# Second attention: stack fills from POOL's queue, and a new written order for each engine's step

## The chip, the cores and the metric

The kernel runs on one core of a Trainium2 chip. A core has a matrix engine (TensorE, here PE), a vector engine (VectorE, DVE), a scalar engine (ScalarE, ACT), a general engine (GpSimd, POOL) and a sync engine (SyncE, SP), which issues most of the DMAs. Each engine works through its own list of instructions in order and waits on semaphores. DMAs issued by SP go into a hardware queue, those issued by POOL into a software queue; both are served by the core's 16 DMA engines. The metric is the time of one execution on the device in microseconds (us), lower is better.

## The reference

Two transformer layers on x of (16, 256, 128), in float32. Each layer normalises x and adds an attention and a mixture of experts. The change lies in the second layer's attention, 16 heads of 8 channels with relative positions clipped at 64 both in the scores and in the values:

```python
dist = jnp.clip(idx[None, :] - idx[:, None], -R, R) + R
pe_k = rel_emb_k[dist]
pe_v = rel_emb_v[dist]
qkv = (x @ W_qkv + b_qkv).reshape(b, s, 3, H, hd)
...
q = q / jnp.sqrt(jnp.asarray(hd, x.dtype))
score = jnp.einsum('bhqd,bhkd->bhqk', q, k) + jnp.einsum('bhqd,qkd->bhqk', q, pe_k)
attn = jax.nn.softmax(score, axis=-1)
ctx = jnp.einsum('bhqk,bhkd->bhqd', attn, v) + jnp.einsum('bhqk,qkd->bhqd', attn, pe_v)
ctx = jnp.transpose(ctx, (0, 2, 1, 3)).reshape(b, s, d)
return ctx @ W_out + b_out
```

The layer's result is x plus this attention plus the experts' output; the experts' rows lie in DRAM (`eo`) when the attention begins, and each token gathers its two rows and adds them with their gates.

## The kernel before

Four stages follow one another: a front stage (first experts, about 0 to 100 us), the first attention (to about 825 us), the second experts (`ffn1_stage`, to about 1100 us) and the second attention (`attn1_stage`, L1331, to the end).

The second attention handles 16 batches of 256 tokens in 32 steps, one for each tile of 128 queries. `steps` (L1374) writes them all out, four to a round r; `tile_of` (L1380) gives the tile within its batch (`it`, 0 or 1) and which of two stack buffers holds the batch (`par`). A step works on eight head pairs (`hp`), and several tiles are in flight at a time:

- PE (`step`, L1499) computes for tile s the key scores of each head pair (`key_scores`, L1428, into the two buffers `ps_S`), for the next tile s+1 the relative scores (`rel_scores`, L1421, into the one buffer `ps_R`), then the transposes of the finished exponentials (`transposes`, L1437, two buffers `ps_T`). For the tile before, s-1, it computes the relative values (`rel_values`, L1446, four quarters in two buffers), the values weighed with the probabilities (`weigh`, L1469), the folds (`folds`, L1480) that add the picked relative values, and the transposed reciprocals (`reciprocals`, L1489); for s-2 the output projection (`project_out`, L1495). Once per batch come `project_qk` (L1405, in it = 1) and `project_v` (L1412, in it = 0).
- ACT (`step`, L1578) copies the relative scores out (`keep_R`, L1553), takes the exponentials (`exponentials`, L1561), copies every second transposed pair (`keep_T`, L1572), the reciprocals (`keep_rdT`) and the projected q and k (`keep_qk`).
- DVE (`step`, L1673) adds key scores and the skewed relative scores and takes the minimum (`add_scores`, L1615), copies the other transposed pairs (`keep_T`, L1667), picks the diagonals of the relative values (`pick_diagonal`, L1630), inverts the sums (`invert`), divides (`divide`), adds the projection (`add_y`) and the two gathered expert rows (`combine`, L1649), and stores the values of a batch (`keep_v`, L1603).
- POOL (`step`, L1736) copies x for project_v (`copy_x`), gathers the expert rows of tile s-2 by two indirect DMAs (`gather`, L1724, after the combine of the tile before), and in it = 1 splits q and k of two batches on into three bf16 parts (`split_qk`, L1247).
- SP (`step`, L1778) sends each quarter of the relative scores to DRAM (`send_band`, L1760, `skew`) and fetches it back shifted by a row's place (`fetch_band`, L1767, into `Sb`); it stores results, sends the parts (`send_parts`, L1266, in it = 1, after the fills of the batch before have landed) and, in it = 0, fills the stacks.

A stack holds q and k of a batch as 72 rows of bf16 (nine products of parts of eight channels): `stack_queries` (L1274) and `stack_keys` (L1283) are three DMAs each of 24 rows of 8 KB from DRAM, 192 KB a DMA, issued for the next batch once its parts are in DRAM. The queries are needed by the relative scores one step on, the keys two steps on. What releases a buffer matters for the order: keep_R of a quarter waits until the same quarter of the tile before has been fetched back, and `combine` waits for both gathers of its tile. The order before is a loop over the head pairs in each engine, with the other work hung on single pairs:

```python
for hp in range(HP):
    if it == 0 and hp == 0:
        pe.wait_ge(keys_in[par], (r + 1) * KSTACK)
    key_scores(s, it, par, hp)
    ...
    rel_scores(s + 1, nit, npar, hp)
    if hp >= LAG:
        transposes(s, hp - LAG)
```

In the expert stage SP also sends the first batch's parts and fills its stacks (`experts`, L1041), while POOL splits the first two batches' q and k and then stores the experts' outputs (L1064).

Of the kernel before, what the change touches and what calls it, by code (L numbers as in the profile page):

```python
# [1001 lines left out]
def ffn1_stage(nc, w0_d, w1_d, wo_d, slots_dram, eo_dram, xn_all, send_ids, sent, ident, x_all, b_out, xnT_all, front, parts, one, bias_q, bias_k):  # L1002
# [11 lines left out]
    with Pool(nc) as m:  # L1014
# [23 lines left out]
        with nc.Block() as block:  # L1038
            @block.sync
            def _(sp):  # L1040
                def experts(half, r):  # L1041
                    for i in range(2):
                        e = r * 2 + i
                        g = slice(half * GH, (half + 1) * GH)
                        sp.wait_ge(o_done, up(half * E + e - 1))
                        sp.dma_start(w[i][:, 0:HID], w0_d[bass.ds(e, 1)]).then_inc(loaded[i], 16)
                        sp.dma_start(w[i][:, VALUE:VALUE + full], w1_d[bass.ds(e, 1), :, 0:full]).then_inc(loaded[i], 16)
                        sp.dma_start(w[i][:, HID + PAD:VALUE], w1_d[bass.ds(e, 1), :, full:HID]).then_inc(loaded[i], 16)
                        sp.dma_start(wo[i][:, 0:HC - 1, :], wo_d[bass.ds(e, 1), 0:full].rearrange("a (c p) d -> p (a c) d", p=P)).then_inc(loaded[i], 16)
                        sp.dma_start(wo[i][UP, HC - 1, :], wo_d[bass.ds(e, 1), full:HID]).then_inc(loaded[i], 16)  # L1050
                        sp.dma_start(xe[i][:, :, :], xs_v[bass.ds(e, 1), :, g, :]).then_inc(loaded[i], 16)
                    if half == 0 and isinstance(r, int):

                        send_parts(sp, front, parts, 0)
                        stack_queries(sp, front, parts, 0, 0)
                        stack_keys(sp, front, parts, 0, 0)

                sp.wait_ge(cleared, 1)
                sp.wait_ge(sent[0], 16 * NT)
                rolled(sp, E // 2, lambda r: experts(0, r))  # L1060
                sp.wait_ge(sent[1], 16 * NT)
                rolled(sp, E // 2, lambda r: experts(1, r))

            @block.gpsimd  # L1064
            def _(pool):
                def experts(half, r):
                    for i in range(2):
                        e = r * 2 + i
                        pool.wait_ge(o_ready, half * E + e + 1)
                        pool.dma_start(eo_v[bass.ds(e, 1), :, half * GH:(half + 1) * GH, :], eo[i][:, :, :]).then_inc(stored[i], 16)  # L1070

                scatter(nc, slots_dram, xn_all, send_ids, 1, range(NT - 2 * TPG, NT - TPG), sent)
                for k in range(2):
                    scatter(nc, slots_dram, xn_all, send_ids, k, range(NT - TPG, NT), sent)
                split_qk(nc.gpsimd, pool, front, one, 0, front.sm["qk_ready"], 1)
                nc.gpsimd.tensor_tensor(x_all[:, :, :], x_all[:, :, :], bc(b_out[:, :], 1, NT), ALU.add).then_inc(biased, 1)
                split_qk(nc.gpsimd, pool, front, one, 1, front.sm["parts_out"], PSENDS)
                pool.wait_ge(sent[1], 16 * NT)
                for half in range(2):
                    rolled(pool, E // 2, lambda r: experts(half, r))  # L1080
                pool.wait_ge(biased, 1)
                for i in range(2):
                    pool.wait_ge(stored[i], 16 * PAIRS1)
# [104 lines left out]
HP = H1 // 2  # L1188
# [11 lines left out]
QUAD = 4  # L1200
# [130 lines left out]
def attn1_stage(nc, front, x_all, xnT_all, a, gates, slot_ids, ident, one, bias_q, bias_k, bias_v, rel_st, tabs, pick, fold):  # L1331
# [6 lines left out]
    LAG = 2  # L1338
    RING = 4
    with Pool(nc) as m:  # L1340
# [61 lines left out]
        with nc.Block() as block:  # L1402
            @block.tensor
            def _(pe):
# [94 lines left out]
                def step(r, i):  # L1499
                    s = r * 4 + i  # L1500
                    it, par = tile_of(i)
                    nit, npar = tile_of(i + 1)
                    pit = 1 - it
                    behind = tiles_behind(r, i)
                    prev_b = r * 2 + par - (1 if it == 0 else 0)
                    for hp in range(HP):
                        if it == 0 and hp == 0:
                            pe.wait_ge(keys_in[par], (r + 1) * KSTACK)
                        key_scores(s, it, par, hp)
                        if it == 1 and hp == 0:  # L1510
                            pe.wait_ge(queries_in[npar], (r + 1 + (1 if i == 3 else 0)) * QSTACK)
                        rel_scores(s + 1, nit, npar, hp)
                        if hp >= LAG:
                            transposes(s, hp - LAG)
                        elif behind >= 1:
                            transposes(s - 1, hp + HP - LAG)
                        if it == 1 and hp == 1:
                            project_qk(r * 2 + par + 2)
                        if behind >= 2 and hp == 1:
                            project_out(s - 2)  # L1520
                        if behind >= 1:
                            if hp == 2:
                                reciprocals(s - 1)
                            if hp in (3, 5):
                                rel_values(s - 1, prev_b, pit, hp - 3)
                                rel_values(s - 1, prev_b, pit, hp - 2)
                            if hp == 4:
                                for q in range(QUAD):
                                    weigh(s - 1, prev_b, pit, q)
                            if hp == 7:  # L1530
                                folds(s - 1)
                        if it == 0 and hp == 7:
                            project_v(r * 2 + par)

                pe.wait_ge(sm["cleared"], 1)
                pe.wait_ge(sm["loaded"], 16 * 3)
# [16 lines left out]
            def _(act):  # L1553
# [24 lines left out]
                def step(r, i):  # L1578
                    s = r * 4 + i
                    it, par = tile_of(i)  # L1580
                    behind = tiles_behind(r, i)
                    for hp in range(HP):
                        keep_R(s + 1, hp)
                        exponentials(s, it, hp)
                        if hp % 2 == 0:
                            if hp >= LAG:
                                keep_T(s, it, hp - LAG)
                            elif behind >= 1:
                                keep_T(s - 1, 1 - it, hp + HP - LAG)
                        if behind >= 1 and hp == 2:  # L1590
                            keep_rdT(s - 1)
                        if it == 1 and hp == 1:
                            keep_qk(nc, act, front, ps_p, bias_q, bias_k, r * 2 + par + 2)

                for hp in range(HP):
                    keep_R(0, hp)
# [5 lines left out]
            def _(v):  # L1602
# [70 lines left out]
                def step(r, i):  # L1673
                    s = r * 4 + i
                    it, par = tile_of(i)
                    behind = tiles_behind(r, i)
                    for hp in range(HP):
                        add_scores(r, i, hp)
                        if hp == 0:
                            if behind >= 2:  # L1680
                                divide(s - 2)
                            if it == 1:
                                keep_v(r * 2 + par)
                        if hp == 1 and behind >= 1:
                            invert(s - 1, 1 - it)
                        if hp % 2 == 1:
                            if hp >= LAG:
                                keep_T(s, it, hp - LAG)
                            elif behind >= 1:
                                keep_T(s - 1, 1 - it, hp + HP - LAG)  # L1690
                        if hp == 1 and behind >= 2:
                            add_y(s - 2)
                        if behind >= 1 and 3 <= hp < 7:
                            pick_diagonal(s - 1, 1 - it, hp - 3)
                        if hp == 7 and behind >= 2:
                            combine(s - 2)

                nc.vector.memset(vx[:, :, :, :, :], 0.0)
                nc.vector.memset(ps_X0[:, :, :, :], 0.0)
# [18 lines left out]
            def _(pool):  # L1718
# [15 lines left out]
                            in_offset=bass.IndirectOffsetOnAxis(ap=ids[:, k, :], axis=0)).then_inc(sm["rows_in"], 16)  # L1734

                def step(r, i):  # L1736
                    it, par = tile_of(i)
                    if it == 1:

                        copy_x(r * 2 + par + 1)  # L1740
                    if tiles_behind(r, i) >= 2:
                        gather(r * 4 + i - 2)
                    if it == 1:

                        split_qk(nc.gpsimd, pool, front, one, r * 2 + par + 2, sm["parts_out"], (r * 2 + par + 2) * PSENDS)
# [9 lines left out]
            def _(sp):  # L1755
# [22 lines left out]
                def step(r, i):  # L1778
# [1 line left out]
                    it, par = tile_of(i)  # L1780
                    nit, npar = tile_of(i + 1)

                    if it == 0:
                        stack_queries(sp, front, parts, r * 2 + par + 1, 1 - par)
                    send_band(s + 1, nit, 0)
                    fetch_band(s, it, 3)
                    if s >= 3:
                        store(s - 3)
                    if it == 0:
                        stack_keys(sp, front, parts, r * 2 + par + 1, 1 - par)  # L1790
                    send_band(s + 1, nit, 1)
                    fetch_band(s + 1, nit, 0)
                    if it == 1:
# [105 lines left out]
```

## Time and profile before

| | |
|---|---|
| median of 3 runs | 1667.84 us (1659.12 to 1680.68) |
| profiled execution, its own time | 1669.93 us |
| its span, first to last instruction | 1668.3 us |
| mean granted TensorE clock | 0.972 of full speed |
| PE busy over the span | 1513.7 us (91%) |
| DVE busy | 905.4 us (54%) |
| ACT busy | 729.8 us (44%) |
| POOL busy | 300.3 us (18%) |
| hardware queue (SP) | 169.54 MB, 39.0% of the 16 DMA engines' span |
| software queue (POOL) | 12.44 MB, 2.6% |

Times in the trace are counted from the first instruction, in us. A busy PE counts from the start of a matmul to its modelled end, and matmuls overlap; where a number should say how long PE needs, the chain's pieces or the distance of two starts is used. An idle time stands in brackets in front of the instruction that ended it, with what ended it.

### The profile page before, as it was taken

The numbers are of one execution on the slowest core, as the hardware profiler recorded it, in microseconds if no ns is written. First come the engines' busy times: TensorE is split into PE (matmuls) and PEld (weight loads), VectorE is DVE, ScalarE is ACT, GpSimd is POOL, SyncE is SP. The second block draws the span as 40 slices with busy tenths as digits, with TensorE's granted clock in tenths as the row PEclk, the third lists the DMA queues.
The fourth block names the chain that finished last, engine by engine and source line by source line (L and its number), as shares of the span: only waits on it lengthen the run. The fifth ranks groups of instructions, "written<-read, shape, count | busy, mean of one in ns | idle before, by whom it ended". The sixth has DMA issues, their size and how long they took to land. (4 is left out here: it accounts for less than half of the span.)

```text
span 1668.3 us, 37746 instructions
## 1 busy us (share of the span) xinstructions
PE 1513.7 (91%) x13904; PEld 1216.0 (73%) x13912; DVE 905.4 (54%) x3195; ACT 729.8 (44%) x1975; POOL 300.3 (18%) x383
## 2 busy tenths in 40 slices
PE   6899999999999999999599999948898989888987
PEld 5568888888888888888365656527677777766776
DVE  5336545454545454545322222226778787767786
ACT  2322222222222222222232232338788888878885
POOL 2011201111010101010440000002333233223333
PEclk9999999999999999999799999968999999999999
DMA  4009400000000000000243232248889998888996
GB/s 119 0 7 86 105 9 8 8 6 7 3 9 3 9 2 10 0 13 1 88 118 114 76 114 76 83 119 230 251 251 259 257 265 258 237 257 232 262 257 200
DMA packets 214008, 183.80 MB, mean 110 GB/s; under 512 B 83275, under 2 KB 203749, under 8 KB 211420
## 3 DMA queue, kind: packets, MB, share of 16 engines
q1 hardware_dynamic: 208494, 169.54, 39.0%
q0 software_dynamic: 5376, 12.44, 2.6%
q8 instruction: 85, 1.39, 0.4%
q14 instruction: 53, 0.43, 0.1%
HBM read 103.63 MB, written 78.14 MB: 109 GB/s over the span
## 5 line engine op out<-in xcount | busy, mean ns | idle before, releaser
L1564 ACT ACTIVATE a1Pm<-a1Pm,a1nmx 128x256 f32<-128x256 f32 x512 | 255.6, 504 | 0.0
L1626 DVE CUSTOM_DVE_ANT_0 a1Pm<-a1ps_S,a1Sb 128x256 f32<-128x256 f32 x512 | 195.9, 420 | 77.6 <-issue 61.2
L775 DVE TENSOR_TENSOR a0AT<-a0ps_AM,mask 128x384 f32<-128x384 f32 x256 | 124.9, 549 | 192.0 <-PE a0ps_AM L595 191.8
L780 DVE TENSOR_TENSOR a0MT<-a0ps_AM,mask 128x384 f32<-128x384 f32 x256 | 138.3, 554 | 87.4 <-PE a0ps_AM L616 86.8
L1559 ACT ACTIVATE a1Rt<-a1ps_R 128x384 f32<-128x384 f32 x264 | 127.9, 485 | 111.1 <-PE a1ps_R L1424 78.3
L1443 PE MATMUL a1ps_T<-ident,a1Pm 128*128 128x128 f32 x1024 | 158.9, 278 | 0.3 <-ACT a1Pm L1564 0.3
L1169 DVE TENSOR_TENSOR f1hid<-f1ge,f1ps_b 128x512 f32<-128x512 f32 x80 | 55.0, 687 | 192.0 <-PE f1ps_b L1102 184.4
L614 PE MATMUL a0ps_AM<-a0AT 128*128 128x256 f32 x512 | 152.9, 380 | 0.0
L1424 PE MATMUL a1ps_R<-rel_st,a1stk 72*128 72x192 bf16 x528 | 91.7, 257 | 65.0 <-ACT a1Rt L1559 49.2
L579 PE MATMUL a0ps_qk<-xnT_all,a0w_in 128*128 (+1 forms) x512 | 138.3, 393 | 2.0 <-PEq L151 1.3
L722 ACT ACTIVATE a0qk<-a0ps_qk 128x512 f32<-128x512 f32 x128 | 76.4, 597 | 116.5 <-PE a0ps_qk L579 116.5
L726 ACT ACTIVATE a0v<-a0ps_v 128x512 f32<-128x512 f32 x64 | 38.2, 597 | 190.6 <-PE a0ps_v L605 190.6
L1443 PEld LDWEIGHTS a1ps_T<-ident,a1Pm 128*128 128x128 f32 x1024 | 117.4, 144 | 0.9 <-ACT a1Pm L1564 0.6
L1424 PEld LDWEIGHTS a1ps_R<-rel_st,a1stk 72*128 72x128 bf16 x528 | 41.7, 99 | 103.6 <-ACT a1Rt L1559 83.1
L730 ACT ACTIVATE a0oT<-a0ps_o 128x512 f32<-128x512 f32 x64 | 38.2, 597 | 171.4 <-PE a0ps_o L628 171.4
L615 PEld LDWEIGHTS a0ps_AM<-a0AT 128*128 128x128 f32 x512 | 97.3, 190 | 13.2
L1112 PE MATMUL f1ps_o<-f1wo,f1hid 128*128 128x128 f32 x768 | 90.0, 277 | 16.4 <-DVE f1hid L1169 16.4
L1433 PE MATMUL a1ps_S<-a1stk 72*128 72x256 bf16 x512 | 102.2, 282 | 0.0
L1112 PEld LDWEIGHTS f1ps_o<-f1wo,f1hid 128*128 128x128 f32 x768 | 87.0, 192 | 20.7 <-DVE f1hid L1169 13.1
L579 PEld LDWEIGHTS a0ps_qk<-xnT_all,a0w_in 128*128 128x128 f32 x512 | 87.1, 190 | 19.9 <-issue 12.1
L1100 PE MATMUL f1ps_a<-f1xT,f1w 128*128 128x512 f32 x192 | 99.8, 602 | 0.7 <-ACT f1xT L1132 0.7
L1564 ACT ACTIVATION_READ_ACCUMULATOR a1Pm<-a1Pm,a1nmx 128x1 f32 x512 | 99.4, 194 | 0.0
(249 smaller groups left out, 2988.9 us busy)
## 6 DMA issues: line engine op xcount, KB each, us to landing
skew<-a1Rt SPq DMA_DIRECT2D x132, 384.0 KB, 5.0
a1Sb<-skew SPq DMA_DIRECT2D x131, 384.0 KB, 5.6
a1stk<-parts_q SPq DMA_DIRECT2D x51, 192.0 KB
a1stk<-parts_k SPq DMA_DIRECT2D x51, 192.0 KB
f1w<-in_L_ffn_w_kernel SPq DMA_DIRECT2D x16, 344.0 KB, 2.9
f1w<-in_L_ffn_w_kernel SPq DMA_DIRECT2D x16, 320.0 KB, 3.2
f1wo<-in_L_ffn_wo_kernel SPq DMA_DIRECT2D x16, 320.0 KB, 4.2
slots<-zeros SPq DMA_DIRECT2D x8, 512.0 KB, 15.0
```

What stands on the lines that cost most here:

```text
L579: ins = nc.tensor.matmul(ps_qk[:, i, :], w_in[:, i, p * P:(p + 1) * P], xnT_all[:, bass.ds(b * T, T)], start=True, stop=True)
L614: nc.tensor.matmul(M[:, 0:T], S[:, 0:P], S[:, 0:T], start=True, stop=True)
L775: nc.vector.tensor_tensor(AT[i][h][:, :], ps_AM[i][h][:, 0:HB], mask[:, :], ALU.mult).then_inc(A_ready, 1)
L780: nc.vector.tensor_tensor(MT[i][h][:, :], ps_AM[i][h][:, 0:HB], mask[:, :], ALU.mult).then_inc(M_ready, 1)
L1100: nc.tensor.matmul(ps_a[u % 2][:, :], w[i][:, u * P:(u + 1) * P], xT[i][:, :], start=True, stop=True).then_inc(a_done, 1)
L1112: ins = nc.tensor.matmul(ps_o[i][:, s, :], hid[:, c, s * P:(s + 1) * P], wo[i][:, c, :], start=(c == 0), stop=(c == HC - 1))
L1424: ins = nc.tensor.matmul(ps_R[:, n, :], stk[par][:, 0, 2 * hp + n, it * P:(it + 1) * P], rel_st[:, it, :], start=True, stop=True)
L1433: ins = nc.tensor.matmul(ps_S[hp % 2][:, n, :], stk[par][:, 0, h, it * P:(it + 1) * P], stk[par][:, 1, h, :], start=True, stop=True)
L1443: ins = nc.tensor.transpose(ps_T[k % 2][:, n, jt, :], Pm[:, place(2 * k + n), jt * P:(jt + 1) * P], ident[:, :])
L1559: nc.scalar.activation(Rt[:, hp, :, :], ps_R[:, :, :].rearrange("p n c -> p c n"), ACT.Copy).then_inc(sm["R_ready"], 1)
L1564: nc.scalar.activation(Pm[:, place(h), :], Pm[:, place(h), :], ACT.Exp, bias=nmx[it][:, h:h + 1], scale=-1.0, accum_out=den[it][:, h:h + 1 ...
L1626: nc.vector.tensor_tensor_reduce(out=Pm[:, place(h), :], in0=ps_S[hp % 2][:, n, :], in1=bias_of(it, hp, n), scale=-1.0, scalar=3.0e38, op0 ...
```

## The change

The six stack fills of a batch move from SP's list to POOL's: in each step with it = 0 POOL waits until the step before has finished its key scores (S_done) and then issues them, ahead of the gather of that step. The first batch's fills move to POOL in the expert stage. PE, ACT and DVE keep their instructions; the loop over head pairs is replaced by a list written out line by line, with relative scores and relative values earlier, and on DVE `divide` first and `combine` between the additions of pairs 3 and 4. The helper functions stay as they are. The diff, with the removed loops cut:

```diff
--- before.py
+++ after.py
@@ -1052,8 +1052,6 @@
         if half == 0 and isinstance(r, int):
 
             send_parts(sp, front, parts, 0)
-            stack_queries(sp, front, parts, 0, 0)
-            stack_keys(sp, front, parts, 0, 0)
 
     sp.wait_ge(cleared, 1)
     sp.wait_ge(sent[0], 16 * NT)
@@ -1075,6 +1073,8 @@
     split_qk(nc.gpsimd, pool, front, one, 0, front.sm["qk_ready"], 1)
     nc.gpsimd.tensor_tensor(x_all[:, :, :], x_all[:, :, :], bc(b_out[:, :], 1, NT), ALU.add).then_inc(biased, 1)
     split_qk(nc.gpsimd, pool, front, one, 1, front.sm["parts_out"], PSENDS)
+    stack_queries(pool, front, parts, 0, 0)
+    stack_keys(pool, front, parts, 0, 0)
     pool.wait_ge(sent[1], 16 * NT)
     for half in range(2):
         rolled(pool, E // 2, lambda r: experts(half, r))
@@ -1500,37 +1500,57 @@
         s = r * 4 + i
         it, par = tile_of(i)
         nit, npar = tile_of(i + 1)
-        pit = 1 - it
+        b = r * 2 + par
+        prev_b = b - (1 if it == 0 else 0)
         behind = tiles_behind(r, i)
-        prev_b = r * 2 + par - (1 if it == 0 else 0)
-        for hp in range(HP):
-            if it == 0 and hp == 0:
...
+        if it == 0:
+            pe.wait_ge(keys_in[par], (r + 1) * KSTACK)
+        key_scores(s, it, par, 0)
+        if it == 1:
+            pe.wait_ge(queries_in[npar], (r + 1 + (1 if i == 3 else 0)) * QSTACK)
+        rel_scores(s + 1, nit, npar, 0)
+        if behind >= 1:
+            transposes(s - 1, 6)
+        key_scores(s, it, par, 1)
+        if behind >= 1:
+            transposes(s - 1, 7)
+        rel_scores(s + 1, nit, npar, 1)
+        if it == 1:
+            project_qk(b + 2)
+        key_scores(s, it, par, 2)
+        rel_scores(s + 1, nit, npar, 2)
+        if behind >= 2:
+            project_out(s - 2)
+        if behind >= 1:
+            rel_values(s - 1, prev_b, 1 - it, 0)
+            rel_values(s - 1, prev_b, 1 - it, 1)
+        transposes(s, 0)
+        rel_scores(s + 1, nit, npar, 3)
+        key_scores(s, it, par, 3)
+        transposes(s, 1)
+        if behind >= 1:
+            reciprocals(s - 1)
+            rel_values(s - 1, prev_b, 1 - it, 2)
+            rel_values(s - 1, prev_b, 1 - it, 3)
+        key_scores(s, it, par, 4)
+        key_scores(s, it, par, 5)
+        rel_scores(s + 1, nit, npar, 4)
+        transposes(s, 2)
+        transposes(s, 3)
+        rel_scores(s + 1, nit, npar, 5)
+        if behind >= 1:
+            for q in range(QUAD):
+                weigh(s - 1, prev_b, 1 - it, q)
+        rel_scores(s + 1, nit, npar, 6)
+        key_scores(s, it, par, 6)
+        transposes(s, 4)
+        transposes(s, 5)
+        rel_scores(s + 1, nit, npar, 7)
+        key_scores(s, it, par, 7)
+        if it == 0:
+            project_v(b)
+        if behind >= 1:
+            folds(s - 1)
 
     pe.wait_ge(sm["cleared"], 1)
     pe.wait_ge(sm["loaded"], 16 * 3)
@@ -1578,19 +1598,33 @@
     def step(r, i):
         s = r * 4 + i
         it, par = tile_of(i)
+        b = r * 2 + par
         behind = tiles_behind(r, i)
-        for hp in range(HP):
-            keep_R(s + 1, hp)
-            exponentials(s, it, hp)
...
+        keep_R(s + 1, 0)
+        if behind >= 1:
+            keep_T(s - 1, 1 - it, 6)
+        keep_R(s + 1, 1)
+        exponentials(s, it, 0)
+        if it == 1:
+            keep_qk(nc, act, front, ps_p, bias_q, bias_k, b + 2)
+        exponentials(s, it, 1)
+        keep_R(s + 1, 2)
+        keep_R(s + 1, 3)
+        exponentials(s, it, 2)
+        if behind >= 1:
+            keep_rdT(s - 1)
+        keep_T(s, it, 0)
+        exponentials(s, it, 3)
+        keep_R(s + 1, 4)
+        keep_T(s, it, 2)
+        keep_R(s + 1, 5)
+        exponentials(s, it, 4)
+        exponentials(s, it, 5)
+        keep_R(s + 1, 6)
+        keep_T(s, it, 4)
+        keep_R(s + 1, 7)
+        exponentials(s, it, 6)
+        exponentials(s, it, 7)
 
     for hp in range(HP):
         keep_R(0, hp)
@@ -1673,27 +1707,38 @@
     def step(r, i):
         s = r * 4 + i
         it, par = tile_of(i)
+        b = r * 2 + par
         behind = tiles_behind(r, i)
-        for hp in range(HP):
-            add_scores(r, i, hp)
-            if hp == 0:
...
+        if behind >= 2:
+            divide(s - 2)
+        if it == 1:
+            keep_v(b)
+        add_scores(r, i, 0)
+        if behind >= 1:
+            keep_T(s - 1, 1 - it, 7)
+            invert(s - 1, 1 - it)
+        add_scores(r, i, 1)
+        if behind >= 1:
+            pick_diagonal(s - 1, 1 - it, 0)
+        add_scores(r, i, 2)
+        if behind >= 2:
+            add_y(s - 2)
+        if behind >= 1:
+            pick_diagonal(s - 1, 1 - it, 1)
+        add_scores(r, i, 3)
+        keep_T(s, it, 1)
+        if behind >= 1:
+            pick_diagonal(s - 1, 1 - it, 2)
+        if behind >= 2:
+            combine(s - 2)
+        add_scores(r, i, 4)
+        add_scores(r, i, 5)
+        if behind >= 1:
+            pick_diagonal(s - 1, 1 - it, 3)
+        keep_T(s, it, 3)
+        add_scores(r, i, 6)
+        keep_T(s, it, 5)
+        add_scores(r, i, 7)
 
     nc.vector.memset(vx[:, :, :, :, :], 0.0)
     nc.vector.memset(ps_X0[:, :, :, :], 0.0)
@@ -1734,12 +1779,18 @@
                 in_offset=bass.IndirectOffsetOnAxis(ap=ids[:, k, :], axis=0)).then_inc(sm["rows_in"], 16)
 
     def step(r, i):
+        s = r * 4 + i
         it, par = tile_of(i)
+        if it == 0:
+            if s > 0:
+                pool.wait_ge(sm["S_done"], s * HP)
+            stack_queries(pool, front, parts, r * 2 + par + 1, 1 - par)
+            stack_keys(pool, front, parts, r * 2 + par + 1, 1 - par)
         if it == 1:
 
             copy_x(r * 2 + par + 1)
         if tiles_behind(r, i) >= 2:
-            gather(r * 4 + i - 2)
+            gather(s - 2)
         if it == 1:
 
             split_qk(nc.gpsimd, pool, front, one, r * 2 + par + 2, sm["parts_out"], (r * 2 + par + 2) * PSENDS)
@@ -1780,14 +1831,10 @@
         it, par = tile_of(i)
         nit, npar = tile_of(i + 1)
 
-        if it == 0:
-            stack_queries(sp, front, parts, r * 2 + par + 1, 1 - par)
         send_band(s + 1, nit, 0)
         fetch_band(s, it, 3)
         if s >= 3:
             store(s - 3)
-        if it == 0:
-            stack_keys(sp, front, parts, r * 2 + par + 1, 1 - par)
         send_band(s + 1, nit, 1)
         fetch_band(s + 1, nit, 0)
         if it == 1:
```

## Rows read from the trace of the kernel before

**Rows 1.** The chain that ended last: start us, us, what.

```profile
1178.76 1.88 PE a1ps_c L1477 x64
...
1590.48 7.71 DMA skew<-a1Rt
1598.20 6.46 DMA a1Sb<-skew
1612.14 1.88 PE a1ps_c L1477 x64
...
1644.50 1.88 PE a1ps_c L1477 x64
```

**Rows 2.** Stretches: us, PE, PEld, DVE, ACT, POOL busy, clock, DMA share, GB/s.

```profile
1300.00:1400.00 100.00, 91.28 (x1340) 73.47 (x1338) 79.92 (x357) 85.29 (x285) 32.05 (x45) 1.00 0.92 261
```

**Rows 3.** The chain within 1300 to 1345 us, pieces of PE.

```profile
1313.31 1.02 PE a1ps_X L1465 x16
1314.34 0.87 PE a1ps_p L1465 x16
...
1332.42 1.08 PE a1ps_c L1485 x32
...
1334.14 0.22 PE a1ps_S L1433 x2
1334.36 0.17 PE a1ps_R L1424 x2
1334.52 0.44 PE a1ps_T L1443 x4
```

**Rows 4.** Timeline of ACT: start us, us, engine, line, out<-in, count [idle before].

```profile
1604.75 0.49 ACT L1559 ACTIVATE a1Rt<-a1ps_R 128x384 f32<-128x384 f32 x1 [1.56 <-DMA a1Sb<-skew]
1605.16 0.51 ACT L1564 ACTIVATE a1Pm<-a1Pm,a1nmx 128x256 f32<-128x256 f32 x1
...
1606.16 0.57 ACT L1575 ACTIVATE a1PT<-a1ps_T 128x512 f32<-128x512 f32 x1
```

**Rows 5.** Timeline of DVE.

```profile
1587.38 0.73 DVE L1657 SCALAR_TENSOR_TENSOR x_all<-a1rows,gates,x_all 128x128 f32<-128x128 f32 x2
...
1597.72 0.42 DVE L1626 CUSTOM_DVE_ANT_0 a1Pm<-a1ps_S,a1Sb 128x256 f32<-128x256 f32 x1 [1.31 <-issue]
...
1598.41 0.69 DVE L1670 COPY a1PT<-a1ps_T 128x512 f32<-128x512 f32 x1
1599.01 0.68 DVE L1636 TENSOR_TENSOR a1X<-a1ps_X,pick 128x512 f32<-128x512 f32 x1
```

**Rows 6.** DMA issues of the page: out<-in, queue, count, KB each, median us to landing.

```profile
skew<-a1Rt SPq DMA_DIRECT2D x132, 384.0 KB, 5.0
a1Sb<-skew SPq DMA_DIRECT2D x131, 384.0 KB, 5.6
```

**Rows 7.** Timeline of PE.

```profile
1597.28 0.39 PE L1433 MATMUL a1ps_S<-a1stk 72*128 72x256 bf16 x2
```

**Rows 8.** Timeline of POOL.

```profile
1576.44 1.04 POOL L1255 TENSOR_TENSOR a1prt<-a1qkf,one 128x512 bf16<-128x512 f32 x1 [1.50 <-ACT a1qkf L1244]
...
1581.17 1.04 POOL L1255 TENSOR_TENSOR a1prt<-a1low,one 128x512 bf16<-128x512 f32 x1
...
1603.37 0.17 POOL L1727 COPY a1ids<-slot_ids 128x2 uint32<-128x2 uint32 x1
...
1605.26 0.95 POOL L1732 DMA_INDIRECT a1rows<-eo,a1ids  x1 [0.30 <-issue]
```

**Rows 9.** Timeline of SP's queue.

```profile
1249.22 0.47 SPq L1271 DMA_DIRECT2D parts_k<-a1prt  x1
...
1253.34 1.44 SPq L1280 DMA_DIRECT2D a1stk<-parts_q  x3
```

**Rows 10.** The line of POOL's plain DMA: duration ns min/median/max, first and last start.

```profile
L1070 POOL DMA_DIRECT2D eo<-f1eo x16: 750/750/857, 852.0 to 1093.8; - x16
```

**Rows 11.** The line of POOL's gather, from its issue.

```profile
DMA to landing us min/median/max: 2.5/5.3/9.6
```

More of the change, by code:

```diff
@@ L1502, in step @@
                     nit, npar = tile_of(i + 1)
-                    pit = 1 - it
+                    b = r * 2 + par
+                    prev_b = b - (1 if it == 0 else 0)
                     behind = tiles_behind(r, i)
-                    prev_b = r * 2 + par - (1 if it == 0 else 0)
-                    for hp in range(HP):
-                        if it == 0 and hp == 0:
[L1508 to L1533, printed above, removed]
@@ L1580, in step @@
                     it, par = tile_of(i)
+                    b = r * 2 + par
                     behind = tiles_behind(r, i)
-                    for hp in range(HP):
-                        keep_R(s + 1, hp)
-                        exponentials(s, it, hp)
[L1585 to L1593, printed above, removed]
+                    keep_R(s + 1, 0)
[23 more added lines that the diff above has]
+                    exponentials(s, it, 7)
                 for hp in range(HP):
@@ L1675, in step @@
                     it, par = tile_of(i)
+                    b = r * 2 + par
                     behind = tiles_behind(r, i)
-                    for hp in range(HP):
-                        add_scores(r, i, hp)
-                        if hp == 0:
[L1680 to L1696, printed above, removed]
+                    if behind >= 2:
+                        divide(s - 2)
```

## The prediction

> **What bounds the kernel now.** The change lies in the second attention, so I read that stage first. The chain of waits gives its pace: the weighing (64 matmuls, 1.88 us) starts at 1178.76 and, 28 steps later, at 1644.50 [rows 1]. That is 465.74 / 14 = 33.27 us for a pair of steps (one batch), 16.6 a step. The table of stretches shows in a quiet 100 us PE busy 91.28, ACT 85.29, DVE 79.92, and the DMA engines at a share of 0.92 [rows 2]. No engine is full by itself, and the reader should expect the bound in the hand-overs between engines that each work through a fixed list.
>
> The chain's pieces tell how long PE really needs, since each counts until the next one's start: key scores S 0.22, relative scores R 0.17, transposes T 0.44, two relative values 1.02 + 0.87, folds 1.08 [rows 3], weighing 1.88 [rows 1]. With eight each of S, R and T, the second pair of relative values at about half (an estimate: half the matmuls) and a projection (from the folds at 1332.42 to the key scores at 1334.14 are 1.72, which leaves 0.64 [rows 3]) a step needs some 13.5 us of PE. ACT: a pair of exponentials E takes 1.00 (1605.16 to 1606.16), a keep_R 0.41 before it, a keep_T some 0.5 [rows 4]; 8 x 1.41 + 4 x 0.5 + 0.4 for what is small is 13.7. DVE: a pair of score additions 0.69, a keep_T 0.60, a pick the same by its length, combine 0.73 [rows 5]; with what is small some 13.2. Each needs about 13.5 and the step takes 16.6: 3 us a step are waits for another list.
>
> One of the waits is for DMAs. At 1604.75 a step's first keep_R had sat idle 1.56 us for a band fetch [rows 4]. The chain shows why: that band went out at 1590.48, took 7.71, and came back in 6.46 [rows 1], where the medians of the two DMAs are 5.0 and 5.6 [rows 6]. SP issues the 1.1 MB of stack fills around it.
>
> **The new order, laid out.** No instruction of PE, ACT or DVE is added or removed, so a gain must come from waits. I lay out a first-tile step from its first key scores (time 0) with the durations above (the number behind a letter is the head pair). A hand-over costs 0.4 to 0.6 from the start of the producing instruction: key scores at 1597.28 [rows 7], their addition at 1597.72 [rows 5].
> PE: T6 of the tile before at 0.4, T7 at 1.4 (after the last exponentials), R1 1.8, R2 2.8, first relative values 3.1 to 5.0, T0 5.0, R3 5.5, T1 5.9, second relative values 6.4 to 7.5, S4 and S5 to 7.9, T2 8.1, T3 8.9, weighing 9.5 to 11.4, T4 and T5 to 12.7, S7 to 13.1, project_v to 13.6, folds to 14.6.
> ACT: keep_R0 1.3, keep_R1 2.2, E0 2.6, E1 3.6, keep_R2 4.5, keep_R3 5.9 (0.9 idle, for R3), E2 6.2, E3 7.8, keep_R4 8.8, keep_R5 9.7, E4 10.1, E5 11.1, keep_R6 12.1, E6 13.4, E7 to 15.4.
> DVE: addition 0.5, keep_T7 2.0, invert 2.6, addition 3.0, pick 4.2, addition 4.8, pick 5.8, addition 6.4, keep_T1 7.2, pick 7.8, **combine 8.4**, additions 9.1 and 9.9, pick 10.7, the last addition to 14.3.
> So 14.64 us. The second-tile step, with keep_v ahead on DVE and the projection of q and k ahead of S2, comes out at 14.51 by the same working and ends with ACT 1.3 us past PE's end, as the first began. A pair takes 29.15; for the small gaps between PE's groups, left out above, I add 0.4: 29.55. Against 33.27 that is 3.7 us a pair, if nothing else moves.
>
> **What the POOL queue costs.** In a first-tile step POOL now waits for the key scores of the step before (0.9 before time 0) and for the parts in DRAM, issues six stack fills, and only then gathers the expert rows that combine wants at 8.4. Before, nothing stood ahead of that gather. The parts: by the layout the split starts 4.0 into the second-tile step; it lasts from 1576.44 to the end of the row at 1581.17, 5.8 [rows 8], so SP sends the parts from 9.8, the last at 10.7. They land at the latest 4.1 later by the closest pair (parts at 1249.22, stack at 1253.34 [rows 9]), which is 0.3 past the next time 0; a fuller queue may make it 2.1. I take 0.8.
> A stack fill on POOL is not in the trace. The nearest row is the only plain DMA that POOL issues, eo, 0.75 [rows 10]. Below it I allow 0.3 (fewer and longer runs, 24 rows of 8 KB); above it, by the gather's row of 0.95 [rows 8], 0.95. I take 0.75 and 0.1 between: six end at 0.8 + 5.1 = 5.9. The gather's ids follow, and its second DMA starts 1.9 later (1603.37 to 1605.26 [rows 8]), at 7.8. Gathers land 2.5 to 9.6 after their issue, median 5.3 [rows 11], and they now also stand behind the stack data in the same queue. I take 3.9, midway between least and median, since the fills have had 7 us to drain: 11.7. Combine is wanted at 8.4, and DVE has 0.6 to spare there (its next addition ends its part 0.6 before E4 can begin). DVE stands still, and with it E4, T4 and all behind: 11.7 - 8.4 - 0.6 = 2.7 us a pair. Bounds: fills at 0.3 with a landing of 2.5 bring the rows at 0.8 + 1.8 + 1.9 + 2.5 = 7.0, no wait; parts at 2.1, fills at 0.85 with their gap and a landing of 5.3 bring them at 14.4, a wait of 5.4.
> The bands: from keep_R1's end to the next step's keep_R0 took 14.3 before (1590.48 to 1604.75 [rows 1, 4]); the layout leaves 12.8, so unchanged latencies would stall 1.5 a pair. The wait at combine comes ahead of that point and covers it. It costs what it says if that cover is gone (rival 2).
>
> **The sum.** 29.55 + 2.7 = 32.25 a pair. The old mean of 33.27 lies 0.9 above a quiet pair (1612.14 to 1644.50 is 32.36 [rows 1]), for late DMAs; as the hardware queue loses the fills and the wait at combine covers such delays, I add none (all of it back would be 14 us). Gain 1.02 x 16 pairs = 16 us. The first batch's fills, now on POOL in the expert stage, cost nothing: POOL's first store there would go out 5 us later (six at 0.85), and its buffer is next needed an expert or two on. What they cost without that cover is those 5 us, once. The profiled run took 1669.9 (span 1668.3), 2.1 above the median of 1667.8: 1669.9 - 16 gives 1654, and I forecast 1653.
>
> **Rivals.**
> 1. No wait at combine, and fast bands. Fills at 0.3 let the gather land before 9.0, and bands at their medians, 5.0 + 5.6 [rows 6], fit into 12.8. Pair 29.55, gain 3.7 x 16 = 60: 1610. For it: POOL is busy 32 of 100 us [rows 2]. Against it: the 0.75 row.
> 2. No wait at combine, but the bands keep their 7.7 and 6.5 beside the fills: pair 29.55 + 1.5 = 31.05, gain 2.2 x 16 = 35: 1635. For it: the bytes stay, and the DMA share is 0.92 in a longer step [rows 2]. Against it again the 0.75 row. Beside it stands a rule of the Trainium skill, "DMA: Bandwidth & Descriptors", section Issuing engines are not separate DMA queues: DMAs of all issuers run on the same 16 DMA engines and interleave, and issuing from several saves only issue time. By that rule moving the fills does not speed the bands; no run here shows it yet.
> 3. The gather comes so late that the kernel is slower. Its place is combine in each first-tile step, its price 5.4 by the bound above: 29.55 + 5.4 = 34.95, 1.7 more than now, x 16 = +27: 1697. It decides from rows landing later than 8.4 + 0.6 + 3.7 = 12.7. For it: landings up to 9.6 occur [rows 11], and the gather stands behind 1.1 MB. Against it: those 7 us.
>
> **How the numbers follow.** Forecast 0.45, rival 1 0.18, rival 2 0.17, rival 3 0.20. The forecast's own range is 1630 to 1675: a landing 1.2 earlier or later moves it by 19. A change of 2% (33 us: below 1634 or above 1701) is about what a measurement of this kernel can tell. Faster by that: rival 1 whole, half of rival 2, a twentieth of the forecast: 0.30. Slower: somewhat over half of rival 3, whose waits can also be longer: 0.12. Same: 0.58. The range leaves out a tenth at each end: 1612 to 1694.
>
> **What would show it.** Right: in first-tile steps DVE idles 2 to 3 us before combine for the DMA of a1rows, in nearly all of them; a fill takes POOL 0.75; second-tile steps take 14.5 to 15; ACT's idle time for a1Sb shrinks. Wrong: no idle time ahead of combine (rivals 1 and 2, told apart by ACT's waits for a1Sb), fills far from 0.75, or steps over 15.5 without a wait at combine, which would put the error into my layout.

## The result and the profile after

The changed kernel takes 1710.18 us (median of 4 runs), the one before 1669.64, measured beside it: a ratio of 1.0241 (95% interval 1.0199 to 1.0284). It is slower by 2.4%, past the upper end of the predicted range (1694). The profiled execution, the longest of the four, took 1720.68 with a span of 1719.1.

The row of stretches that answers to [rows 2] (same columns):

```profile
1300.00:1400.00 100.00, 82.99 (x1095) 68.03 (x1094) 68.63 (x300) 72.89 (x239) 35.29 (x55) 0.90 0.85 227
```

PE, DVE and ACT each do less in 100 us (1095 PE instructions for 1340; over 1150 to 1650 us 5895 for 6444), the granted clock is 0.90 instead of 1.00, and the DMA engines are less busy. So all of them wait more. For whom, the waits over 1150 to 1700 us say (engine, line, whom it waited for: us in all, times, longest):

```profile
DVE x_all L1691 <- DMA a1rows<-eo,a1ids: 81.9, 15, 7.2
...
POOL a1stk L1280 <- PE a1ps_S L1433: 43.5, 9, 5.7
```

and over 1150 to 1650 us, with the bands, the kernel before first:

```profile
ACT a1Rt L1559 <- DMA a1Sb<-skew: 26.1, 18, 4.1
```

```profile
ACT a1Rt L1579 <- DMA a1Sb<-skew: 31.6, 7, 4.9
```

The first row is DVE ahead of `combine`: 81.9 / 15 = 5.5 us in nearly every batch; the kernel before has no such wait in this stretch. The last is ACT waiting for a band: 7 times instead of 18, but 4.5 us each instead of 1.5. The second, POOL's own, is the time for which it stands idle until its fills may go. One batch on POOL's timeline, with DVE's row of the same batch below it:

```profile
1299.94 1.60 POOL L1280 DMA_DIRECT2D a1stk<-parts_q  x3 [5.52 <-PE a1ps_S L1433]
1301.52 1.48 POOL L1289 DMA_DIRECT2D a1stk<-parts_k  x3
1303.63 1.04 POOL L1777 DMA_INDIRECT a1rows<-eo,a1ids  x1 [0.16 <-issue]
1304.98 0.97 POOL L1777 DMA_INDIRECT a1rows<-eo,a1ids  x1 [0.30 <-issue]
```

```profile
1313.83 0.74 DVE L1691 SCALAR_TENSOR_TENSOR x_all<-a1rows,gates,x_all 128x128 f32<-128x128 f32 x2 [5.98 <-DMA a1rows<-eo,a1ids]
```

The six fills leave within 3.06 us, 0.5 each, faster than I thought. The second gather is issued at 1304.98, and its rows are there only at 1313.83, 8.85 us later. DVE had stopped at 1307.85. The page's DMA issues show what lies in front of it (median us to landing at the end), beside the bands that answer to [rows 6]:

```profile
skew<-a1Rt SPq DMA_DIRECT2D x132, 384.0 KB, 4.4
a1Sb<-skew SPq DMA_DIRECT2D x131, 384.0 KB, 4.3
...
a1stk<-parts_k POOLq DMA_DIRECT2D x51, 192.0 KB, 8.8
```

The keys' fills land 8.8 us after their issue (median), and the gather issued behind them lands with them: in this batch the last fill at 1313.45 and the two gathers at 1312.99 and 1313.81, by the trace's landings. The bands' medians fell (from 5.0 and 5.6), yet the chain of waits shows what a median hides:

```profile
1516.64 3.21 DMA skew<-a1Rt
1519.87 12.57 DMA a1Sb<-skew
1533.57 3.57 PE a1ps_c L1477 x64
```

One fetch, issued just as the fills of its step went out (POOL's row there is 1518.99), took 12.57. Most bands travel undisturbed, and some in each batch meet all six fills: of the 220 sends and fetches from 1150 to 1650 us 47 took over 9 us, three or four in a batch, and in the kernel before 23 of 240. (These two counts go by the landing events of the trace, the last one before the same quarter's next DMA, for all four quarters; the page's medians leave out the quarters whose events are not complete.) The last row is the weighing, 3.57 instead of 1.88. The stretches around one of DVE's stops (it ended at 1605.68, after 6.73) tell why:

```profile
1604.00:1608.00 4.00, 0.65 (x3) 0.18 (x3) 2.28 (x13) 1.19 (x5) 0.00 (x0) 0.76 0.71 245
1608.00:1612.00 4.00, 3.91 (x21) 3.15 (x25) 3.18 (x13) 3.13 (x12) 0.08 (x1) 0.50 0.40 108
```

PE was busy for 0.65 of 4 us, and in the next 4 us it works at a granted 0.50, the lower level of 1.2 GHz. So here a stall costs its own length and some slow microseconds behind it.

### The profile page after: what moved, and what is told of

The parts are those of the page before. It is cut to its first block and busy times, and to the rows that moved or that the text cites. A ratio compares the mean times of both kernels' runs of the same rounds, so it can differ in the third digit from the quotient of the medians.

```text
span 1719.1 us, 37761 instructions
## 1 busy us (share of the span) xinstructions
PE 1542.2 (90%) x13904; PEld 1245.3 (72%) x13912; DVE 919.6 (53%) x3195; ACT 737.8 (43%) x1975; POOL 353.6 (21%) x485
## 5 line engine op out<-in xcount | busy, mean ns | idle before, releaser
L1424 PEld LDWEIGHTS a1ps_R<-rel_st,a1stk 72*128 72x128 bf16 x528 | 47.0, 102 | 88.6 <-ACT a1Rt L1579 64.1
L616 PE MATMUL a0ps_AM<-a0AT 128*128 128x128 f32 x512 | 99.0, 275 | 0.0
```

The source lines that it names most:

```text
L1424: ins = nc.tensor.matmul(ps_R[:, n, :], stk[par][:, 0, 2 * hp + n, it * P:(it + 1) * P], rel_st[:, it, :], start=True, stop=True)
```

## The experiments

Theory A: the gather behind the fills is the loss. B: the fills in their own queue hold up a band fetch in flight. C: the new order gains nothing. D, added after the first four runs: it is the size of the fills' packets, which take turns with the bands' packets of 1536 bytes. E, added with it: it is how much is asked for at once. All ratios are to the kernel before, measured beside the run. Waits of ACT for bands and of DVE for rows are told from the list of waits over 1150 to 1650 us.

**gather_first**: in first-tile steps the gather goes ahead of the fills.

```diff
+if it == 0 and tiles_behind(r, i) >= 2:
+    gather(s - 2)
 if it == 0:
...
-if tiles_behind(r, i) >= 2:
+if it == 1 and tiles_behind(r, i) >= 2:
     gather(s - 2)
```

> The changed kernel with one edit: in first-tile steps POOL issues the gather ahead of the six stack fills. Theory A (the loss is the gather standing behind the fills: 81.9 us of DVE idle before combine between 1150 and 1700 us, plus a granted clock of 0.50 for some us after each idle stretch): 1620 to 1650, DVE's idle time before combine under 10 us in total, the stage's granted clock back at 0.97 or more. Theory B (the fills on a queue of their own hold up a band fetch in flight, 12.5 us instead of 6.5, and ACT stands still for it whatever combine does): 1680 to 1710, ACT's idle time for a1Sb rises from 31.6 to over 60. Theory C (the written order gains nothing by itself): 1660 to 1675 with neither wait.

Measured 1703.73, ratio 1.0175 (1.012 to 1.023). The wait at combine fell from 84.1 us in the whole stage to 2.1, and almost nothing was won, since ACT's wait for bands doubled, as B expected (1680 to 1710, over 60 us):

```profile
ACT a1Rt L1579 <- DMA a1Sb<-skew: 61.0, 15, 5.7
```

Its chain has in one batch

```profile
1436.89 3.32 DMA skew<-a1Rt
1440.23 12.76 DMA a1Sb<-skew
```

and its fills were issued at 1439.37 to 1442.42, around that fetch. The end of this fetch in the stretches:

```profile
1450.00:1452.00 2.00, 0.00 (x0) 0.00 (x0) 0.00 (x0) 0.00 (x0) 0.00 (x0) 1.00 0.68 187
1454.00:1458.00 4.00, 4.00 (x68) 3.33 (x68) 1.69 (x6) 2.51 (x10) 0.00 (x0) 0.50 0.81 223
```

No engine does anything for 2 us, only the DMA engines run; then PE goes on at 0.50. A alone falls: with the wait at combine gone, the wait for bands takes its place.

**order_only**: the new order, but the fills back on SP (queries' ahead of the first band, keys' behind the store, as before).

```diff
-stack_queries(pool, front, parts, r * 2 + par + 1, 1 - par)
-stack_keys(pool, front, parts, r * 2 + par + 1, 1 - par)
...
+if it == 0:
+    if s > 0:
+        sp.wait_ge(sm["S_done"], s * HP)
+    stack_queries(sp, front, parts, r * 2 + par + 1, 1 - par)
 send_band(s + 1, nit, 0)
```

> The changed kernel with the fills of the stacks back in SP's list at their old places, the queries' now behind a wait for the key scores of the step before; the new order of PE, ACT, DVE stays and POOL's gather has nothing ahead of it. Theory A: 1620 to 1650, since the gather is early. Theory B: 1620 to 1650 too, since there is one queue again and no fetch over 10 us in first-tile steps. Theory C: 1660 or more.

1654.40, 0.9894 (0.9859 to 0.9928). C, which expected 1660 or more, falls: the order alone gains 1.1%. A and B both expected at most 1650, so it misses their range by 4, and the longest fetch took 11.4 where B expected none over 10. ACT waits 42.5 us for bands, in 28 waits of 1.5 each.

**fills_only**: the loops of before, with POOL's fills ahead of the gather.

> The kernel before with only the fills moved to POOL, ahead of the gather, behind the wait for the key scores; the loops over head pairs stay, so combine stands last in a step. Theory A: 1655 to 1680: rows landing 14 us into a step of 16.6 are just in time for combine, under 15 us of DVE idle time before it. Theory B: 1690 to 1720 with ACT's idle time for a1Sb over 60 us (27.7 before). Theory C: at or below 1665, as the queue would have been the useful part.

1675.42, 1.0034 (1.0001 to 1.0066), by itself next to no change. A's range (1655 to 1680) holds; B's (1690 or more, over 60 us of waits for bands) does not. Still, ACT's wait for bands rose from 26.1 to 55.8, with fetches of 9 to 12 us in the chain; combine, which comes later in that order, hardly waits (2.1 over the stage):

```profile
ACT a1Rt L1559 <- DMA a1Sb<-skew: 55.8, 20, 5.2
```

If the two parts added up, the change would give 0.9894 x 1.0034 = 0.993. It gives 1.024. The new order asks for the rows sooner, just where the fills make them late (combine_last shows this); that it is the same with the bands is my reading, and no run moves them alone.

**combine_last**: the changed kernel with `combine` moved behind the last addition of DVE's step.

> The changed kernel with one edit: on DVE, combine stands behind the last score addition of the step in place of between additions 3 and 4; POOL keeps the fills ahead of the gather. Theory A: 1630 to 1665, the wait at combine shrinks from 5.5 us a batch to under 2. Theory B: 1680 to 1710, with ACT waiting for a1Sb. Theory C: 1660 to 1675 without either wait.

1680.17 over ten executions, of which one of 1696.22 is left out of the ratio of 1.004 (1.0009 to 1.007). That gives back 30 us of the 40 lost, between A's range (to 1665) and B's (from 1680). No wait at combine is left between 1150 and 1650 us, and ACT waits for bands:

```profile
ACT a1Rt L1579 <- DMA a1Sb<-skew: 42.3, 15, 5.1
```

This run and gather_first both take the wait at combine away, and the fills go out at the same place of the step in both. Why one gives back 30 us and the other 6 stays open.

**small_runs**: gather_first, each fill split into two DMAs with runs of 1 KB.

```diff
+for half in range(2):
+    sp.dma_start(half_heads(front.stk[par][rows, 0, :, :], half), half_heads(q_rows, half))
```

> The kernel with the gather first, each fill cut into two DMAs of alternate pairs of heads, so that its runs are 1 KB in place of 8 KB (12 DMAs, the same bytes). Theory D (packets: the software queue moved the fills in packets of 4096 B, by the counts of the queues, 4896 more packets for 20.06 MB, the bands' are 1536 B, and taken in turn with them a band in flight gets about a quarter of the DMA engines): the longest fetches fall from 12 to 14 us to under 10, ACT's idle time for a1Sb from 61 to under 40 us, the time to 1660 to 1685. Theory E (burst: 1.1 MB asked for within 3 us hold up whatever is in flight, however they are cut): fetches stay at 11 or more, ACT's wait over 50, the time 1695 or more.

1673.66, 1.0026 (0.9998 to 1.0053): 30 us less than gather_first, as D expected (1660 to 1685), while the longest fetch, 11.7, is E's (11 or more). The software queue in the changed kernel and here (packets, MB, share):

```profile
q0 software_dynamic: 10272, 32.50, 7.4%
```

```profile
q0 software_dynamic: 15168, 32.53, 8.0%
```

Before it held 5376 packets and 12.44 MB. Dividing bytes by counts, as the expectations did, gives packets of 4096 bytes for the fills, but the trace has the size of every packet, and there they are 2448 of 8192 bytes, from POOL and from SP alike; the other packets are of 4 bytes. In this run they are 4896 of 4096 bytes, so the edit halved them. It also takes POOL 7 us instead of 3 to issue them (twelve at 0.58), so this run does not tell D from E. ACT still waits 41.5 us for bands, between what D (under 40) and E (over 50) expected.

**fills_split**: gather_first, but the keys' fills, which are needed a step later, go out in the second-tile step.

```diff
 if it == 0:
...
     stack_queries(pool, front, parts, r * 2 + par + 1, 1 - par)
-    stack_keys(pool, front, parts, r * 2 + par + 1, 1 - par)
+if it == 1:
+    pool.wait_ge(sm["S_done"], s * HP)
+    stack_keys(pool, front, parts, r * 2 + par + 1, 1 - par)
```

> The kernel with the gather first, the keys' fills moved one step on, to the start of the second-tile step (behind the wait for the step's key scores before), so that POOL asks for 0.58 MB at a time. Theory D: a band beside either half is still slowed while it lasts, but half as long: longest fetches 8 to 10 us, 1655 to 1685, twice as many slow fetches. Theory E: the same or better, 1645 to 1670, as no burst is over 0.58 MB.

1632.52, 0.9777 (0.9733 to 0.9821): faster than both kernels, with the same bytes, packets and queue as gather_first. Its waits:

```profile
DVE x_all L1691 <- DMA a1rows<-eo,a1ids: 16.7, 16, 2.2
...
ACT a1Rt L1579 <- DMA a1Sb<-skew: 7.5, 7, 2.2
```

ACT's wait fell from 61.0 to 7.5 and no fetch takes over 9.3. Of 241 sends and fetches 4 took over 9 us, by the count used above; in gather_first it was 51 of 220. The packets are as large as there, so their size alone (D) does not decide. The direction is E's, but the time lies below both ranges (D from 1655, E from 1645).

**sp_burst** and **sp_keys_late**: the new order on SP's queue, once with all six fills together, once with the keys' three behind the fetch of the second band.

> The new order with the fills on SP, all six issued together at the start of a first-tile step in place of three and three. Theory D: the fetch issued just before them stays under 8 us, since it is ahead in one queue, the sends behind them take 9 to 12 us, and the time stays within 15 us of the 1654 of the order alone: 1645 to 1670. Theory E: a band in flight takes 11 us or more and the time is 1690 or more.

> The new order with the fills on SP, the keys' fills moved from the second to the third quarter of the step (after the fetch of the second band). Theory D: bands of the first quarters have less ahead of them in the queue, ACT's idle time for a1Sb falls from 42.5 to 25 or less, 1635 to 1652. Theory E: the same, 1635 to 1652. Without an effect (the waits move on to the later bands): 1650 to 1660.

sp_burst took 1695.43, 1.0156 (1.0114 to 1.0199), much like gather_first: a burst does much the same harm from either queue. That is E's range (1690 or more) and not D's (1645 to 1670), and 43 of its 229 sends and fetches took over 9 us, where order_only had 23 of 241. sp_keys_late took 1648.16, 0.9879 (0.9827 to 0.993), within the range that D and E share; its interval overlaps with that of order_only. It has 37 waits for bands, none over 2.2, and 3 of 240 took over 9.

**sp_split**: the twin of fills_split on SP's queue.

```diff
+if it == 1:
+    sp.wait_ge(sm["S_done"], s * HP)
+    stack_keys(sp, front, parts, r * 2 + par + 1, 1 - par)
 send_band(s + 1, nit, 0)
```

> The new order with the fills on SP's hardware queue, the queries' three in the first-tile step and the keys' three in the second-tile step; the twin of fills_split (1632.5) on the other queue. Theory E (what counts is how much is asked for at once): between 1630 and 1645, below order_only (1654) and sp_keys_late (1648), with fewer than 20 waits of ACT for a1Sb in the list of waits and no fetch over 10 us. Theory D (the size of a packet, 4096 bytes on the software queue, 5461 on the hardware queue, decides what a band in flight suffers): SP's larger packets cost more than POOL's, so 1650 or above. A third way: SP's own instruction time, three issues of 0.47 us ahead of the first band of each step, costs the band, and the time comes out near order_only.

1653.05, 0.9889 (0.9854 to 0.9923): near order_only, the third way of the expectation. D expected 1650 or above too, from larger packets on SP's queue; the packets are the same, so that reason falls. E's 1630 to 1645 does not hold. Only 3 of 241 sends and fetches took over 9 us, the longest 10.0, but ACT waits for bands 31 times, 34.5 in all. SP's list shows one reason for which the bands go late:

```profile
1430.81 2.57 SPq L1289 DMA_DIRECT2D a1stk<-parts_k  x3
1433.42 0.38 SPq L1811 DMA_DIRECT2D skew<-a1Rt  x1
```

The band is sent as soon as SP gets to it, 2.6 us after the fills began; one of the three issues took 1.75. Who waits for whom on SP's line of `send_band` sums it up, sp_split first, then fills_split:

```profile
SPq L1811 <- ACT a1Rt L1579: 28.9, 35, 2.3
```

```profile
SPq L1820 <- ACT a1Rt L1579: 99.2, 77, 2.9
```

With the fills on POOL, SP is ready before ACT 77 times, otherwise 35 times. So POOL's queue does buy something: room in SP's list, once the burst is gone. It is not shown to be all: the sends of the first two quarters, which SP issues behind the fills, also take longer from issue to landing here (medians 8.1 and 7.5, by the trace's landing events) than in fills_split (7.1 and 5.5), and no run takes the two apart.

**split_behind**: fills_split with the gather behind the queries' fills again.

> fills_split with the gather of first-tile steps put behind the queries' three fills again; in second-tile steps it was behind the keys' three already. If a gather behind half a batch's fills comes in time: 1630 to 1637, the wait of DVE for a1rows at combine under 25 us in all. If the gather behind any fills in its queue is what costs at combine (theory A in full): a wait of 2 to 3 us in each first-tile step, 16 x 2.5 = 40 us of waits at combine, and 1650 to 1665.

1648.39, 0.9863 (0.9827 to 0.99). The wait at combine:

```profile
DVE x_all L1691 <- DMA a1rows<-eo,a1ids: 48.5, 29, 4.7
```

So A holds as a part: half a batch's fills ahead of the gather cost 16 us against fills_split, just short of what A expected in full (from 1650), while no wait for a band is left in ACT's list. This run is also the changed kernel with the split alone: that gives 62 us, with the gather still behind the fills.

**loops_split**: fills_split's POOL list with the loops of before.

> The order of before (loops over head pairs), the fills on POOL, gather first, queries' and keys' fills in different steps; apart from the order it is fills_split. If the split and the new order add up: fills_only lost 0.3 per cent against before, the new order alone gave 1.1 per cent, so 1650 to 1662 here, with fetches in the chain under 9 us. If the new order is what makes use of the split: 1664 to 1675, no better than before. If the split alone is the whole of the gain: 1628 to 1640.

1640.18, 0.9818 (0.9787 to 0.9849), at the end of the range for the split as the whole of the gain (1628 to 1640): it gives most of it. By the medians the new order adds 8 us, though the intervals overlap.

**spread**: fills_split with the three fills of a step paced by the key scores.

> fills_split with its three fills of a step not asked for together but paced by the key scores: the queries' at the 0th, 2nd and 4th pair of the first-tile step, the keys' at the 0th, 1st and 2nd of the second-tile step. Theory E carried on (smaller bursts are always better): 1615 to 1628, longest fetch below 8.5 us. If half a batch's fills at once is already no burden: 1629 to 1637. Rival: the spread fills meet two or three bands in place of one, and the keys' delay the split of q and k: 1638 or above.

1638.73 (median of three), 0.9817 (0.977 to 0.9864); a fourth execution, left out, took 4846 us, and why stays open. Smaller bursts are not better still; the rival's 1638 or above is met: ACT's wait for bands fell to 1.7, but combine waits 32.5, 16 times. The intervals of this run and of loops_split overlap with that of fills_split; which of them is best stays open.

## Why the prediction was wrong

**The layout held, nearly.** The prediction gave an undisturbed pair 29.55. In fills_split, where no long wait is left, the weighings of the chain stand at

```profile
1378.30 1.88 PE a1ps_c L1477 x64
...
1408.47 1.89 PE a1ps_c L1477 x64
...
1438.64 1.89 PE a1ps_c L1477 x64
```

that is 30.17 a pair, twice, so the layout was 0.6 short of a quiet pair. But what I compared it with was wrong. With the loops of before and the fills split the chain has

```profile
1171.40 1.88 PE a1ps_c L1477 x64
...
1202.71 1.88 PE a1ps_c L1477 x64
...
1233.91 1.88 PE a1ps_c L1477 x64
```

31.2 to 31.3 a pair. These are quiet pairs. Over all 32 steps, from the first and last start of the weighing (1143.4 to 1660.1 before, 1140.2 to 1631.5 in loops_split, 1145.3 to 1622.2 in fills_split), the mean pairs are 33.2, 31.6 and 30.7. Of the 33.27 that I set out to shorten by 3.7, some 1.6 were thus the fills' doing, and the old order itself had 0.9 to give; with the fills left on SP the new order gained 17 us in all (order_only), where 3.7 a pair would be 59. I had read 1.56 us of idle time for a band as one wait among others; the 7.71 and 6.46 of [rows 1] stood beside the fills that SP issued around them, and with the fills split such waits are rare (ACT's 26.1 became 8.6 in loops_split).

**The cost of POOL's queue: right place, wrong term.** The step of the batch shown above begins on PE's timeline with

```profile
1299.32 0.39 PE L1433 MATMUL a1ps_S<-a1stk 72*128 72x256 bf16 x2
```

Counted from there, the first fill starts at 0.6 (I had the parts at 0.8), and DVE stops at 8.5 (I had combine at 8.4). The second gather goes out at 5.7 where I had 7.8, as a fill takes 0.5 and not 0.75. The rows are there at 14.5 where I had 11.7: they come 8.85 after their issue where I took 3.9, "since the fills have had 7 us to drain". That is the step that failed: the landing of the gather. The issue was earlier and the landing later than I had them. In gather_first, with no fills ahead, the second gather of first-tile steps lands 4.9 after its issue (median) instead of 8.8, and the wait is gone; so the landing is set by the fills' data and not by POOL's time. The median of 5.3 in [rows 11], below which I went, also mixes both kinds of step: before, the second gather took 7.6 in first-tile steps and 5.1 in the others. The wait at combine was to be 3.3 with DVE's 0.6 to spare; it is 5.3 (84.1 in 16). Rival 3 had this place, and a price of 5.4 behind the same 0.6; its 1697 is still 13 short, for what follows.

**"The wait at combine comes ahead of that point and covers it."** I gave a band 7.7 and 6.5 beside the fills, priced the stall at 1.5 a pair, and let the wait at combine hide it. Fetches that met the burst took 12.5, and ACT waited 4.5 us seven times beyond the wait at combine. In gather_first the cover was gone, and the price was 61.0 / 15 = 4.1 a batch, not 1.5.

**Nothing was set down for the clock.** After the stops shown PE comes back at 0.50; the stage ran at 0.92 over 1150 to 1650 us and before at 0.99 (before first):

```profile
1150.00:1650.00 500.00, 445.65 (x6444) 359.91 (x6444) 387.18 (x1735) 413.85 (x1378) 154.29 (x206) 0.99 0.90 253
```

```profile
1150.00:1650.00 500.00, 429.85 (x5895) 353.02 (x5884) 364.26 (x1575) 384.59 (x1260) 183.82 (x274) 0.92 0.84 233
```

The sum, from the first and last weighing of the changed kernel:

```profile
L1477 PE MATMUL a1ps_c<-a1PT,a1vx x2048: 272/273/423, 1149.1 to 1711.9; 128*32 128x128 f32 x187
```

(1711.9 - 1149.1 - 1.9) / 15.5 = 36.2 a pair, 3.95 over the predicted 32.25, or 63 us in 16 pairs. Of this 0.6 is the layout, by its quiet pair, and 2.0 the wait at combine (5.3 for 3.3). The other 1.35 is what is left for bands and slow clock, which I did not separate.

Rival 2 had its time (1635) and its missing wait at combine wrong, but it was right that moving the fills does not speed the bands. Its rule of the Trainium skill ("DMA: Bandwidth & Descriptors", Issuing engines are not separate DMA queues), that issuing from several engines only saves issue time, agrees with sp_burst and gather_first (1.0156 and 1.0175, one burst from two issuers). It agrees with fills_split against sp_split too (0.9777, 0.9889), if what was saved there is the issue time of a list in which bands stand behind the fills, which is shown only in part.

## What to carry to other kernels

In this kernel the transfers that were not urgent were best asked for in two portions, in different steps; what mattered was how much was in flight when an urgent one started, whichever queue it came from. Where two waits are met in one step, take away each alone and both together before judging either: here the gather first gave 6 us by itself, the split by itself (split_behind) 62, and the two together 78. And before a new order is priced against the old one, look for what disturbs the old one: most of what was to be had lay in the fills, and the loops of before get it too (1640).

## What was not expected of the hardware

A fill takes POOL 0.50 to 0.61 us, nearly always the same, while on SP in sp_split the median is 0.37 and single ones took up to 1.94. The medians of the bands said the opposite of the truth: 4.3 for a fetch in the slow kernel, 5.9 in the fastest (fills_split) on their pages, and 4.5 and 5.5 where all four quarters are counted. The longest alone does not tell either: 12.0 on the page of the slow kernel, but 12.4 on that of the kernel before. How many are long does tell: 47 of 220 over 9 us in the slow kernel, 23 of 240 before, 4 of 241 in the fastest. Why a fetch of 384 KB needs 12.5 us beside 1.15 MB of fills, where 9.3 is the most beside half of them, was not taken apart into packets, queue and order of service.
